# A third slot for stack fronts and evenly spread maximum products in the later 4-head attentions

## The reference

```python
Q = relu(q @ Wq + bq); K = relu(k @ Wk + bk); V = relu(v @ Wv + bv)     # q = k = v = enc
scores = einsum('hbqd,hbkd->hbqk', Qh, Kh) / sqrt(dh)                   # 4 heads, 1024 x 1024
scores = where(key_mask == 0, NEG, scores)
attn = softmax(scores, axis=-1) * query_mask
out = einsum('hbqk,hbkd->hbqd', attn, Vh) ... + q
return _layer_norm(out, gamma, beta)
```

## Time and profile before

| | |
|---|---|
| median of three runs | 1566.38 us |
| span of the profiled execution (first to last instruction) | 1562.7 us |
| PE busy over the span | 1342.9 us (86%) |
| DVE, ACT, POOL busy | 1070.4, 749.0, 530.2 us |
| mean granted TensorE clock | 0.937 of full speed |
| chain of waits: POOL's queue at L1085 (the adds of the two later attentions) | 18% |

### The profile page before, as it was taken

The page is one execution under the profiler, slowest core; times in us unless marked ns, Lnnn a source line. Parts: engine busy times, 40 slices in busy tenths (PEclk is TensorE's granted clock), DMA queues, the critical chain, the costliest instruction groups (busy, mean ns, idle before and its releaser), DMA issues.

```text
span 1562.7 us, 21716 instructions
## 1 busy us (share of the span) xinstructions
PE 1342.9 (86%) x7242; PEld 768.5 (49%) x7242; DVE 1070.4 (68%) x2665; ACT 749.0 (48%) x1048; POOL 530.2 (34%) x448
## 2 busy tenths in 40 slices
PE   5869998999779979888999989799998788788896
PEld 3513333333268856544444356344443677445796
DVE  4677777777565357776567768675767888676654
ACT  5405555555767445623334435223443734345664
POOL 3001111111241042306776622178865257001212
PEclk8959999999989989989999989799999889899998
DMA  7952333330000000464422305724400020730001
GB/s 252 263 124 46 58 58 58 58 58 2 7 22 1 1 1 34 135 196 95 95 47 49 114 32 185 194 49 95 95 28 1 27 35 24 161 64 3 1 1 54
DMA packets 79849, 110.29 MB, mean 71 GB/s; under 512 B 16576, under 2 KB 55674, under 8 KB 77946
## 3 DMA queue, kind: packets, MB, share of 16 engines
q1 hardware_dynamic: 79737, 108.91, 28.0%
HBM read 70.55 MB, written 37.80 MB: 69 GB/s over the span
## 4 chain that ended last, share of the span: by engine, by line
PE 40%; POOLq 19%; DVE 17%; issue 11%; ACT 6%; DVEq 3%; SPq 2%; DMA 2%; POOL 1%; ACTq 0%
POOLq L1085 18%; PE banks L1556 5%; PE banks L1196 5%; PE banks L1541 5%; PE banks L1138 4%; PE banks L2107 3%; DVE max_parts L1370 3%; PE banks L1171 3%; PE banks L571 2%; DVE mask_rows L1366 2%; PE banks L2137 2%; DVE scratch L1366 2%; PE banks L1149 1%; PE banks L2655 1%; DMA stacks<-neg_max_parts 1%
## 5 line engine op out<-in xcount | busy, mean ns | idle before, releaser
L1331 ACT ACTIVATE x_feat<-banks,key_bias 128x1024 f32<-128x1024 f32 x160 | 176.2, 1114 | 263.7 <-PE banks L1178 203.7
L1084 POOL TENSOR_TENSOR x_feat<-x_feat 128x1024 f32<-128x1024 f32 (+1 forms) x112 | 242.7, 2167 | 95.9 <-ACT x_feat L1331 87.4
L1138 PE MATMUL banks<-stacks 128*128 128x512 f32 (+4 forms) x640 | 230.3, 407 | 37.9 <-DVE max_parts L1359 13.6
L1196 PE MATMUL banks<-x_feat,v_group 128*32 128x512 f32 (+4 forms) x1312 | 230.9, 568 | 8.6 <-ACT x_feat L1331 4.8
L1331 ACT ACTIVATE x_feat<-banks 128x1024 f32<-128x1024 f32 (+2 forms) x224 | 178.8, 840 | 121.8 <-PE banks L1171 120.0
L1138 PEld LDWEIGHTS banks<-stacks 96*128 96x128 bf16 (+1 forms) x640 | 77.2, 139 | 229.1 <-DVE max_parts L1359 92.5
L1108 POOL TENSOR_SCALAR_AFFINE_SELECT x_feat<-x_feat 128x256 f32<-128x256 f32 x128 | 53.7, 420 | 291.4 <-ACT x_feat L1331 290.0
L1171 PE MATMUL banks<-stacks 99*128 99x512 bf16 (+3 forms) x512 | 131.2, 346 | 24.2 <-ACT x_feat L1331 13.9
L1359 DVE CUSTOM_DVE_ANT_0 scratch<-banks,mask_rows 128x512 f32<-128x512 f32 x128 | 88.2, 689 | 49.4 <-PE banks L1138 49.3
L1177 PE MATMUL banks<-stacks 128*128 128x512 f32 x256 | 110.9, 433 | 9.5 <-DMA stacks<-neg_max_parts_r 9.5
L1541 PE MATMUL banks<-stacks 128*128 128x512 f32 x384 | 101.0, 401 | 9.3 <-DVE stacks L1523 8.5
(11 more groups left out here) (295 smaller groups left out, 2470.7 us busy)
## 6 DMA issues: line engine op xcount, KB each, us to landing
stacks<-q_parts_r SPq DMA_DIRECT2D x18, 512.0 KB, 12.1
stacks<-k_parts_r SPq DMA_DIRECT2D x18, 512.0 KB, 14.0
q_parts_r<-stacks SPq DMA_DIRECT2D x16, 512.0 KB, 3.0
k_parts_r<-stacks SPq DMA_DIRECT2D x16, 512.0 KB, 3.5
v_group<-v SPq DMA_DIRECT2D x14, 512.0 KB, 14.5
stacks<-q_parts SPq DMA_DIRECT2D x16, 384.0 KB, 5.2
w_even<-in_w SPq DMA_DIRECT2D x4, 1024.0 KB, 6.6
stacks<-q_parts SPq DMA_DIRECT2D x16, 256.0 KB, 5.5
```

Of the source, the lines that this page charges most:

```text
L1084: e.tensor_tensor(total, total, p, ALU.add)
L1138: m = e.matmul(PS[:, bank, at:at + wide], q[0:rows, h, qt * P:(qt + 1) * P], keys[0:rows, h, k0:k0 + wide], start=True, stop=True, skip_gr ...
L1196: m = e.matmul(PS[w * h:w * (h + 1), bank, t.q0:CH], V[:, h, :], PB[:, t.index % 2, h // 2, h % 2, 0:CH - t.q0], start=t.first, stop=t.las ...
L1331: e.activation(dst, PS[:, 2 * (st % 2):2 * (st % 2) + 2, 0:CH - t.q0], ACT.Exp, scale=A.scale, bias=bias).then_inc(s.p_ready, 1)
```

## The change

The stacks of a later attention are no longer two whole slots. Query and key fronts have three places in turn (`FRONTS`, by g % 3), the third of them (`third_fronts`) on offsets 0 to 4095 of `w_even`; the backs have two places (`BACKS`, by g % 2), which with the first two fronts cover the old slots exactly. With a third front the maximum products of group g+2 can be computed while group g still runs, and `order` spreads them by `places64` over the steps 13 to 15 of group g and 0 to 12 of group g+1, in proportion to a table of how much room a step has on DVE. Group 1's products keep their place in group 0 (steps 6 to 12, newly weighted). The products in each step are, by group:

| group | steps 0 to 15 before | sum | steps 0 to 15 now | sum |
|---|---|---|---|---|
| 0 | 4 3 3 3 3 0 5 5 4 5 4 5 4 0 0 0 | 48 | 4 3 3 3 3 0 6 5 6 4 3 3 5 2 2 3 | 55 |
| 1 | 0 0 0 0 0 4 4 4 4 4 4 4 4 0 0 0 | 32 | 1 3 1 2 2 2 3 2 3 1 2 1 2 2 3 3 | 33 |
| 2 | 0 0 0 0 0 4 4 4 4 4 4 4 4 0 0 0 | 32 | 2 0 2 1 0 3 3 2 3 2 2 2 2 0 0 0 | 24 |
| 3 | none | 0 | none | 0 |

SP loads the fronts of group 2 right behind group 1, ahead of the first maximum rows. Later it sends the maximum rows of the next group, loads the backs and values of group g+2 when group g has ended, and then the fronts of group g+3. The two feed-forward matrices of the last block are loaded three stages later (`load_block3_forward`, beside the index transfer of the stage behind the second later attention).

These are products of group 3, from the first front place again, in steps that held none. The diff, cut to its core:

```diff
     XT = sb("x_feat", [P, NT * D])
-    WA = sb("w_even", [P, 6656])
+    with nc.sbuf_tensor("w_even", [P, 6656], F32) as WA:
+        pass
+    THIRD = sb("third_fronts", [P, 4096], F32R)
+    sb("behind_third_fronts", [P, 6656 - 4096])
     WB = sb("w_odd", [P, 4096])
...
         e.dma_start(RA[:, :, :], a["rows23"].partition_broadcast(P)).then_inc(ld.w3, 16)
-        for w, n in ((W3.w1, "w3_1"), (W3.w2, "w3_2"), (W3.out, "w3_out")):
-            e.dma_start(w, kp(a[n])).then_inc(ld.w3, 16)
+        e.dma_start(W3.out, kp(a["w3_out"])).then_inc(ld.w3, 16)
         e.wait_ge(ld.cleared, 1)
...
         e.dma_start(MI[0:SC, B * SC:B * SC + B], a["mask"].rearrange("b s -> s b"), allow_slow_non_contiguous=True).then_inc(ld.w3, 16)
-    W3_LOADS = 4 + 24 + 2
+    W3_LOADS = 2 + 24 + 2
+
+    def load_block3_forward(e):
+
+        for w, n in ((W3.w1, "w3_1"), (W3.w2, "w3_2")):
+            e.dma_start(w, kp(a[n])).then_inc(ld.w3_ff, 16)
...
             o[start - (A.dh == 64)].append(("M", 0, 0))
-        if r + A.ahead < A.n:
+        if A.halved:
+            for dg in (1, 2):
+                for idx, x in places64(A, r, dg, products(dg), start, span):
+                    o[idx].append(x)
+        elif r + A.ahead < A.n:
             for x in products(A.ahead):
...
         return o
+
+    def places64(A, r, dg, items, start, span):
+
+        g = r + dg
+        if g >= A.n:
+            return []
+
+        def room(of, idx):
+            used = {0: 700, 2: 700, 3: 1000, A.nt0 + 1: 700, A.nt0 + 2: 700, A.nt0 + 3: 1000, span: 1000}.get(idx, 0)
+            if A.norm is not None and of == A.n // B:
+                used += {1: 2100, 4: 2100, 7: 700}.get(idx, 0)
+            return 2100 - used
+        steps = [(0, idx) for idx in range(start, span)] if g == 1 else \
+            [(g - 2, idx) for idx in range(span, A.nt)] + [(g - 1, idx) for idx in range(span)]
+        total, at, found = sum(room(*x) for x in steps), 0, []
+        for of, idx in steps:
+            first, at = at, at + room(of, idx)
+            lo, hi = (-(-len(items) * x // total) for x in (first, at))
+            found += [(idx, x) for x in items[lo:hi] if of == r]
+        return found
...
-    def slot64(A, u):
-
-        if A.self:
-            return [STK1[:, u * 8192 + 2048 * i:u * 8192 + 2048 * (i + 1)].rearrange("p (h n) -> p h n", h=2)
-                    for i in range(4)]
-        q = [STK1[:, u * 4096 + 2048 * i:u * 4096 + 2048 * (i + 1)] for i in range(2)]
-        return [x.rearrange("p (h n) -> p h n", h=2) for x in q] + \
-            [STK1[:, 12288 + 1024 * i:12288 + 1024 * (i + 1)].rearrange("p (h n) -> p h n", h=8) for i in range(2)]
+    FRONTS = [STK1[:, 0:2048], STK1[:, 4096:6144]], [STK1[:, 8192:10240], STK1[:, 12288:14336]], \
+        [THIRD[:, 2048 * i:2048 * (i + 1)] for i in range(2)]
+    BACKS = [[STK1[:, 8192 * u + 4096 * i + 2048:8192 * u + 4096 * (i + 1)] for i in range(2)] for u in range(2)]
+
+    def stack64(g):
+
+        (qa, ka), (qb, kb) = FRONTS[g % 3], BACKS[g % 2]
+        return [x.rearrange("p (h n) -> p h n", h=2) for x in (qa, qb, ka, kb)]
+
+    def front_loaded(g):
+        return (g // 3 + 1) * 64 + 64 * (g % 3 == 0)
...
-    def low_loaded(A, g):
-        return (g // A.slots + 1) * 48 + 32 * (slot_of(A, g) == 0)
+    def low_loaded(g):
+        return (g // 2 + 1) * 48 + 32 * (g % 2 == 0)
...
-        sem = A.s.loaded[u]
+        sem = A.s.loaded[u if A.dh == 16 else g % 3]
         if A.dh == 16:
...
-                    e.dma_start(dst, src).then_inc(A.s.loaded[u + 2] if A.self and piece >= 2 else sem, 16)
+                    e.dma_start(dst, src).then_inc(A.s.loaded[3 + g % 2] if piece >= 2 else sem, 16)
...
-        e.wait_ge(s.loaded[u], loaded_value(A, 0, g))
-        if A.self and A.dh == 64:
-            e.wait_ge(s.loaded[u + 2], low_loaded(A, g))
+        if A.dh == 16:
+            e.wait_ge(s.loaded[u], loaded_value(A, 0, g))
+        else:
+            e.wait_ge(s.loaded[3 + g % 2], low_loaded(g))
...
-                dst, src = slot64(A, u)[1][64 + part:65 + part].bitcast(F32), MPR[0:16, g % 3, part, :].bitcast(F32)
+                dst, src = stack64(g)[1][64 + part:65 + part].bitcast(F32), MPR[0:16, g % 3, part, :].bitcast(F32)
...
-        e.wait_ge(s.loaded[0], loaded_value(A, 0, 0))
-        if A.dh == 64:
-            e.wait_ge(s.loaded[2], low_loaded(A, 0))
+        if A.dh == 16:
+            e.wait_ge(s.loaded[0], loaded_value(A, 0, 0))
+        else:
+            e.wait_ge(s.loaded[0], front_loaded(0))
+            e.wait_ge(s.loaded[3], low_loaded(0))
...
             send_maximum_rows(e, A, g)
+        if A.halved:
+            load_group(e, A, 1, 1)
+            load_group(e, A, 2, 0, (0, 1))
+            send_first_rows(e, A, 1)
+            for g in range(A.n - 1):
+                send_rows(g + 1)
+                if g + 2 < A.n:
+                    e.wait_ge(s.pv_tile, (g + 1) * A.nt)
+                    load_group(e, A, g + 2, g % 2, (2, 3))
+                if g + 3 < A.n:
+                    load_group(e, A, g + 3, (g + 1) % 2, (0, 1))
+            return
         first = 1 if A.self else 2
...
             load(g)
-        if A.halved and not A.first_in_front:
-            send_first_rows(e, A, 0)
-        if not A.window and not A.halved:
+        if not A.window:
             send_rows(0)
...
             load(g)
-        if A.halved:
-            send_first_rows(e, A, 1)
         for g in range(A.n - 1):
...
             if k == 0:
-                e.wait_ge(s.loaded[v], loaded_value(A, i, r + dg))
+                if A.dh == 16:
+                    e.wait_ge(s.loaded[v], loaded_value(A, i, r + dg))
+                else:
+                    e.wait_ge(s.loaded[(r + dg) % 3], front_loaded(r + dg))
             kind, h, qt, half = A.chunks[k]
-            q, keys = slot16(A, v) if A.dh == 16 else slot64(A, v)[0::2]
+            q, keys = slot16(A, v) if A.dh == 16 else stack64(r + dg)[0::2]
             rows = K16 if A.dh == 16 else P
...
             if A.self and A.dh == 64:
-                e.wait_ge(s.loaded[slot_of(A, r) + 2], low_loaded(A, r))
+                e.wait_ge(s.loaded[3 + r % 2], low_loaded(r))
             if A.halved and r == 0:
...
         e.dma_start(IDX, a["idx"].rearrange("b t -> (b t)").partition_broadcast(P)).then_inc(ld.masks, 16)
+        load_block3_forward(e)
         nxt()
...
         e.wait_ge(ld.w2, 64)
+        e.wait_ge(ld.w3_ff, 32)
         e.wait_ge(ld.w3, 16 * W3_LOADS)
```

19 lines of the change are left out of this document (7 added, 12 removed).

## The result

The changed kernel takes 1573.55 us (median of 20 runs, 1568.85 to 1576.44), the kernel before 1567.01 (20 runs): a ratio of 1.0033, 95% interval 1.0022 to 1.0044. It is slower by 6.5 us of the medians (5.2 by the ratio) where 7.6 us of gain were forecast. The profiled execution has a span of 1571.8 us and a mean granted clock of 0.937, as before.

The account below looks back on a forecast made before the run. PE was taken to bound the kernel, waiting for banks in steps of four products. Terms 1.6 + 1.3 - 1.5 - 5.2 = -3.8 us an attention, -7.6 for both, took 1566.4 to 1558.8 us; range 1552 to 1567.

Parts of the forecast that it names:

- Group 2, -5.2 us an attention: Group 2: fewer products in steps 5 to 12 save 5.9 us, early steps cost 0.7; bounds -3 and -8.
- The stall of the layer norm I leave as it is: Group 2: PE's 2.35 us idle behind DVE's scales, then about 4 us at half clock, were taken as unchanged.
- the stall of group 2 disappears: Rival, group 2: lighter steps 6 and 7 end the stall, another -3 us an attention, 1553 us; chance 0.10.
- The first rows, +1.3 us: Group 0, ahead of step 8: rows land at about 733.5, PE is ready at 732.2 and waits 1.3 us.
- half a microsecond: Group 0: the first rows' assumed landing time behind the end of the large transfers at 733.
- The rows come too late, and the gain is given back: Rival, group 0: PE waits 3.3 us and loses about 2 to the clock; 1567 us, no change; chance 0.15.
- twice their pace: Rival, group 0: rows land from 738 on, 14 us for four transfers; 1572 us, slower than before; chance 0.09.
- Group 0's products, +1.6: Group 0, steps 13 to 15: seven products of group 2 at 0.23 us each add 1.6 us an attention.
- Group 1, -1.5: Group 1: moved products save 2.7 us, waits on DVE in steps 3 and 13 take 1.2; bounds 0 and -4.
- POOL takes over: Rival: evenly filled steps run at POOL's pace, costing group 1's gain, 1561.8 us; chance 0.14 with the rest.
- The weights, 0: Two weight matrices, 2 MB needing 9 us, loaded later where transfer engines idle for 32 us: no cost.
- wrong if group 2 keeps 53 us (then the bank waits were not what made it long): The prediction's own test on group 2's length, which it expected to be 48 to 50 us.

Follow-up runs that it names:

- e10: e1 without the layer norm's additions, moments and scales on DVE in group 2, but for one small instruction each; ratio to before 0.9891.
- e11: e5 without the layer norm's additions, moments and scales on DVE in group 2, but for one small instruction each; ratio to before 0.9912.
- e2: Changed kernel with the maximum products back in their old places, first rows still behind group 2's fronts; ratio to before 1.0042.
- e5: Changed kernel with the maximum products back in their old places and the first rows issued ahead of group 2's fronts; ratio to before 0.9971.
- e1: Changed kernel with the first maximum rows of the second query half issued ahead of group 2's fronts; ratio to before 1.0011.
- e12: e4 with no products in step 13 of group 0, so that M stands there alone; 1563.3 us, ratio to before 0.9963.
- e9: e1 with POOL's adds of all tiles but the first of a half on a quarter of the columns only; ratio to before 0.9850.
- e4: Changed kernel with first rows ahead of group 2's fronts and no products in steps 5 and 8 of group 2; 1558.35 us, ratio to before 0.9939.

## Why the prediction was wrong

**Group 2, -5.2 us an attention: the step that failed.** The prediction said "The stall of the layer norm I leave as it is" and counted products alone. For products alone it was not far off: -4.2 (e10 against e11). But the stall was no constant. In the old order PE stood 1.7 to 2.4 us behind the scales and at most 0.75 behind the moments (before, e2, e5): four products followed these too, but DVE met only the end of a POOL add there. In the new order DVE met a whole add, and PE stood behind the moments as well. The layer norm's price rose from 4.6 and 3.9 us (before less e11) to 8.6 and 7.8 (e1 less e10), and the whole term became -0.2 and -1.4, beyond the -3 that was its bound for a grown stall. The rows to see it stood in the trace: POOL busy for 40 of 54 us in group 2, and small DVE instructions that take many times as long as their like: L414 on 128x4 1.29 us and 0.16 at 837.08, L1429 on 128x8 1.92 us and 0.17 at 819.18. The rival "the stall of group 2 disappears" went the other way.

**The first rows, +1.3 us: mis-sized.** Moved by the 3.3 us that the trace starts later, the forecast had the queue empty at 736.3 and PE ready at 735.5; measured are 736 and 735.9. The rows released PE about 1.9 us behind the end of the large transfers and not half a microsecond, so the wait was 2.06 and 2.69 us, and the clock fell, at 0.8 and 1.2: 2.8 and 3.9 in sum. The half microsecond had no row behind it; the 1.8 us of 8 KB on an idle queue, which the prediction read itself, would have given a wait of 733 + 1.8 - 732.2 = 2.6. The rule on ring order in the Trainium skill's "DMA: Bandwidth & Descriptors", section "Queues, rings and completion order", is borne out: the rows, issued from 1029.98 on in the second attention, were there only behind the last front (1039.27). The rival "The rows come too late, and the gain is given back" named the mechanism, a wait and a fallen clock; its price, 3.3 and about 2 us, was above the 2.8 and 3.9 measured, it was given 0.15, and there was little gain to give back. In the next rival, "twice their pace" is a slip: 14 us for four transfers is 1.5 times the 9.2 us read.

**Group 0's products, +1.6: too small by 0.9.** Seven products and M cost +2.5 (e1 against before). With six of them and M alone it is +1.8 (e12), 0.3 each. M between the scores was priced only in group 1; in group 0 PE waits 1.08 us for it as well (L1186 at 760.86).

**Group 1, -1.5: right,** measured -1.1 and -2.5. Of the second, 1.4 is the wait for fronts that the third place takes away, a gain that the prediction did not list.

**POOL takes over: excluded** as a pace, for groups 0 and 1 by e9 and for group 2 by e10. POOL did matter, not as a pace but as what blocks DVE.

**The weights, 0: nothing speaks against it.** e5, with the weights moved, is faster than before.

The sum, by the runs: late rows +2.8 and +3.9; seven products and M +2.5; group 1 -1.1 and -2.5; group 2 -0.2 and -1.4: +4.0 and +2.5, the 6.5 us measured. The prediction's own test, "wrong if group 2 keeps 53 us (then the bank waits were not what made it long)", fired, but its reading was wrong: spreading the products did save 4.2 us (e10 against e11), and a new wait took their place.

What stays open: why the clock falls after a wait in one execution and not after the same wait in another, which makes group 2 of the old order vary between 51.9 and 54.0 us (before, e2, e5); what fixes whether DVE's addition meets the start or the end of a POOL add; and how e4 and e12 compare.
